# Three weight units without a part of x, and two steps in another order, in a gated-experts kernel

## The chip, the core and the metric

The kernel runs on one core of one Trainium2 chip. The metric is device time in microseconds (us), from the start to the end of one execution. Shown are the median of three runs and one execution taken by the hardware profiler, whose trace all rows below come from. The engines are PE (TensorE matmul), PEld (its weight loads), DVE (VectorE), ACT (ScalarE), POOL (GpSimd) and SP (SyncE); the last two only issue transfers here.

## What is computed

x has 512 rows of 64 positions with 768 columns. A score per position (x times aw) is turned into a softmax over the 64 positions, and the weighted sum of the positions is the feature of the row. The feature goes through four gate networks and eight experts of two layers; each row takes the gate of its own head D, and the experts' outputs are summed with that gate.

```python
p = softmax(where(x.sum(-1) != 0, einsum('bld,d->bl', x, aw), -inf))
feature = einsum('bl,bld->bd', p, x)
g_all = softmax(relu(feature @ gW1[h] + gb1) @ gW2[h] + gb2);  gate = g_all[arange(b), D]
h1 = relu((feature @ eW1[e] + eb1) * inv1 + bn1_b)
h2 = relu((h1 @ eW2[e] + eb2) * inv2 + bn2_b)
rep = einsum('be,ebo->bo', gate, h2)
out = softmax((rep @ hW[h] + hb)[arange(b), D])
```

## The kernel before

x is read in 32 **rounds** of 16 rows (8 tiles of 128 positions x 768). DVE multiplies each tile by aw and sums it (`score_tiles`, L626, tile prod_out); ACT sums each tile for the mask (`sum_rows`, L429, copy_out). Then DVE masks the scores (`mask_scores`, L632, L636), PE transposes them (`turn_scores`, L915), DVE takes the maximum (`softmax_max`, L641, neg_max), ACT the exponential (L436), DVE normalises (`softmax_norm`, L647 recip and L649 prob), PE transposes the result (`turn_probs`, L919), ACT spreads it into pwin (`place_probs`, L447), and PE adds the weighted rows to the feature sum (`add_features`, L937, 32 matmul rows in the trace). Eight rounds make a block of 128 rows. After a block ACT and DVE each copy half of the sum (`copy_rows`, L452, L655), PE transposes it (`turn_features`, L950), ACT and DVE split it into a high and a low part (`features_hi` L457, `features_lo` L661).

The batch is worked in two chunks of 256 rows. The weights of a chunk come in **units** of 128 x 3 x 384 elements, 56 for each chunk, 112 in all. Nearly every unit is split in two parts: ACT writes whi (`split_hi`, L414), DVE the rest wlo (`split_lo`, L614), and PE makes three products for each tile: 27 matmuls a unit (L875, L876, L877). The second-layer units of the first three experts of chunk 0 are not split (L906). The first-layer output h1 of an expert is split by DVE the same way, in two halves (`split_h1`, L682 h1_hi and L684 h1_lo). `add_expert` (L702, L706) multiplies an expert's output by its gate and adds it to rep; `pick_gate` (L692) readies the gate's broadcast, which PE makes (L961). POOL issues the weights' transfers into four raw buffers, each as soon as `split_lo` has read the buffer's last unit (L394); SP issues those of x into a ring of four rounds, each when `add_features` has freed a round.

The program has two stretches. The first works rounds 0 to 15 with x alone. The second has one **slot** for each unit: 112 slots, written out by hand in each engine's queue. In slot s PE multiplies unit s, while ACT and DVE split unit s + 2 (AHEAD = 2; there are three pairs of split buffers, so `split_hi(s + 2)` waits until PE has used unit s - 1). The slots also carry x: each takes a third of a round (three, three and two tiles), so rounds 16 to 31 end in slot 46. Which third a slot carries is

```python
SLOT_THIRD = THIRDS * FIRST_ROUNDS + 1
r, third = divmod(SLOT_THIRD + s, THIRDS)
```

(L147; L562 for ACT, L832 for DVE, L1025 for PE). Third 0 has the masking, and on PE `add_features` of two rounds earlier and then `turn_scores`; third 1 has the maximum and the exponential; third 2 has `softmax_norm` on DVE and, behind the unit on PE, `turn_probs`. So PE's queue waits in every third slot for DVE's L649.

In a DVE slot the order is: first tile, the softmax step, `split_lo(s + 2)` (L847), `split_h1` where H1_SLOT has one (L848), the other tiles, then `gate_norm`, `gate_set`, `pick_gate`, `add_expert`. Chunk 0 has slots 0 to 55. Its second-layer units of expert 7 are units 54 and 55; unit 56 is the first gate unit of chunk 1, and PE waits before it for the features of blocks 2 and 3. Block 3 is complete with round 31, whose sum PE makes in slot 50 (BLOCK_SLOT, L153). The gate of a chunk takes five steps in the slots behind its eight gate units: logits, copy, pick, norm, set (L139). PE transposes the gate behind the unit of the slot in which DVE makes the norm (`turn_gate`, L997, waits for L761), and DVE sets it in the next slot (`gate_set`, L771, L773). HEAD_SLOT = gate_at(1) + 12 is where PE makes chunk 0's last product.

Of the kernel before, what the change touches and what calls it, by code (L numbers as in the profile page):

```python
# [21 lines left out]
BLOCK_ROUNDS = 8  # L22
RAW = 4
SPLIT = 3
AHEAD = 2
# [8 lines left out]
THIRDS = 3  # L34


def rec_kernel(nc, x, D, aw, gW1, gb1, gW2, gb2, eW1, eb1, bn1_g, bn1_b, eW2, eb2, bn2_g, bn2_b, hW, hb, out):
    B, L, DM = x.shape
    H, _, HD = gW1.shape
# [4 lines left out]
    CB = CHUNK // P  # L44
    NBLK = B // P
    ROUNDS = NBLK * BLOCK_ROUNDS
# [7 lines left out]
    with ExitStack() as ctx:  # L54
# [22 lines left out]
        SLOTS = len(UNITS)  # L77
# [58 lines left out]
        def gate_at(c):  # L136
            return unit_of(c, "g", 0, 0)

        GATE_LOGITS, GATE_COPY, GATE_PICK, GATE_NORM, GATE_SET = (  # L139
            {gate_at(c) + n: c for c in range(NCH)} for n in (2 * H, 2 * H + 1, 2 * H + 2, 2 * H + 3, 2 * H + 4))  # L140
        HEAD_SLOT = gate_at(1) + 2 * H + 4

        FIRST_ROUNDS = CB * BLOCK_ROUNDS
        SLOT_THIRD = THIRDS * FIRST_ROUNDS + 1  # L147

        def to_score(third):
            return range(3 * third, min(3 * third + 3, ROUND_TILES))  # L150


        BLOCK_SLOT = {THIRDS * (BLOCK_ROUNDS * (b + 1) + 1) - SLOT_THIRD: b for b in range(CB, NBLK)}  # L153
        assert max(BLOCK_SLOT) + 3 < gate_at(1)

        xring = sb("xring", [P, RING_ROUNDS, CG, 2, DM])
        aw_bc = sb("aw_bc", [P, DM])
# [246 lines left out]
        def _(act):  # L404
# [154 lines left out]
                features_hi(1, g)  # L559

            for s in range(SLOTS):
                r, third = divmod(SLOT_THIRD + s, THIRDS)  # L562
                if s - 1 in BLOCK_SLOT:
                    copy_rows(BLOCK_SLOT[s - 1])
                if r <= ROUNDS:
                    split_hi(s + AHEAD)
                if s:
                    read_panel(s - 1, (2,))
                if r > ROUNDS:
                    split_hi(s + AHEAD)  # L570
                if s - 2 in BLOCK_SLOT:
                    for g in range(2):
                        features_hi(BLOCK_SLOT[s - 2], g)
                if s in GATE_NORM:
                    gate_exp(GATE_NORM[s])

                ts = to_score(third) if r < ROUNDS else ()
                sum_rows(r, ts[:1])
                if third == 0 and FIRST_ROUNDS <= r - 2 < ROUNDS:
                    place_probs(r - 2)  # L580
                sum_rows(r, ts[1:2])
                if third == 1 and FIRST_ROUNDS < r <= ROUNDS:
                    softmax_exp(r - 1)
                sum_rows(r, ts[2:])
                read_panel(s, (0, 1))
                if s == HEAD_SLOT + 1:
                    head_exp(0)
# [4 lines left out]
        def _(dve):  # L592
# [17 lines left out]
            def split_lo(u):  # L610
                if u >= SLOTS or not is_split(u):
                    return
                dve.wait_ge(hi_ready, SPLITS[u])
                nc.vector.tensor_tensor(wlo[:, split_slot(u), :, :], wraw[:, raw_slot(u), :, :],  # L614
                                        whi[:, split_slot(u), :, :].bitcast(F32), ALU.subtract).then_inc(lo_ready, 1)

            def score_tiles(r, ts):
                for t in ts:
                    j, i = divmod(t, 2)
                    if i == 0:  # L620
                        dve.wait_ge(x_loaded[r % RING_ROUNDS][j], x_count(r))
                    at = r * ROUND_TILES + t
                    if at >= 2:

                        dve.wait_ge(scored, at - 1)
                    nc.vector.tensor_tensor_reduce(  # L626
                        out=prod_out[:, t % 2, :], in0=xring[:, r % RING_ROUNDS, j, i, :], in1=aw_bc[:, :], scale=1.0,
                        scalar=0.0, op0=ALU.mult, op1=ALU.add, accum_out=score[:, r % 2, t:t + 1]).then_inc(scored, 1)
# [37 lines left out]
            def split_h1(c, q, half):  # L666

                n = SPLIT_EXPERT_AT[(c, q)]
                if n and q == 0:

                    dve.wait_ge(logits_ready, c + 1)
                elif n:
                    pc, pq = SPLIT_EXPERTS[n - 1]
                    wait_unit_used(dve, unit_of(pc, "c", pq, half))
                elif NATIVE:

                    wait_unit_used(dve, unit_of(0, "c", NATIVE - 1, 1))
                else:
                    dve.wait_ge(logits_ready, 1)
                dve.wait_ge(z_read, tiles(panel_of(c, "ab"[half], q), MT - 1))  # L680
                ks = slice(KU * half, KU * half + KU)
                nc.vector.tensor_copy(h1_hi[:, ks, :], h1[:, ks, :]).then_inc(h1_hi_ready, 1)  # L682
                dve.wait_ge(h1_hi_ready, h1_count(c, q, half))
                nc.vector.tensor_tensor(h1_lo[:, ks, :], h1[:, ks, :], h1_hi[:, ks, :].bitcast(F32),  # L684
                                        ALU.subtract).then_inc(h1_ready, 1)
# [79 lines left out]
            def gate_set(c):  # L765
                dve.wait_ge(gate_turned, c + 1)
                if c:

                    dve.wait_ge(gate_bc_ready, E * c)

                nc.vector.tensor_copy(gateT[0:E, :], turn_ps[0:E, 0:CHUNK]).then_inc(gateT_hi_ready, 1)  # L771
                dve.wait_ge(gateT_hi_ready, c + 1)
                nc.vector.tensor_tensor(gateT[LOW:LOW + E, :], turn_ps[0:E, 0:CHUNK], gateT[0:E, :].bitcast(F32),  # L773
                                        ALU.subtract).then_inc(gateT_ready, 1)
# [54 lines left out]
                features_lo(1, g)  # L829

            for s in range(SLOTS):
                r, third = divmod(SLOT_THIRD + s, THIRDS)  # L832
                if s in GATE_COPY:
                    gate_copy(GATE_COPY[s])
                if s in GATE_PICK:
                    gate_pick(GATE_PICK[s])
                if s - 1 in BLOCK_SLOT:
                    copy_rows(BLOCK_SLOT[s - 1])
                ts = to_score(third) if r < ROUNDS else ()
                score_tiles(r, ts[:1])  # L840
                if third == 0 and r <= ROUNDS:
                    mask_scores(r - 1)
                if third == 1 and FIRST_ROUNDS < r <= ROUNDS:
                    softmax_max(r - 1)
                if third == 2 and FIRST_ROUNDS < r <= ROUNDS:
                    softmax_norm(r - 1)
                split_lo(s + AHEAD)  # L847
                for c, q, half in H1_SLOT.get(s, ()):  # L848
                    split_h1(c, q, half)
                score_tiles(r, ts[1:])  # L850
                if s - 2 in BLOCK_SLOT:
                    for g in range(2):
                        features_lo(BLOCK_SLOT[s - 2], g)
                if s in GATE_NORM:
                    gate_norm(GATE_NORM[s])
                if s in GATE_SET:
                    gate_set(GATE_SET[s])
                if s == HEAD_SLOT + 1:
                    head_pick(0)

                    nc.vector.memset(rep[:, :, :], 0.0).then_inc(rep_zeroed, 1)
                if s == HEAD_SLOT + 2:
                    head_norm(0)
                if s in PICK_SLOT:
                    pick_gate(*PICK_SLOT[s])
                if s in ADD_SLOT:
                    add_expert(*ADD_SLOT[s])
# [5 lines left out]
        def _(pe):  # L873
# [148 lines left out]
            turn_features(1)  # L1022

            for s in range(SLOTS):
                r, third = divmod(SLOT_THIRD + s, THIRDS)  # L1025
                if s in (gate_at(c) for c in range(NCH)):

                    pe.wait_ge(feat_ready, 2 * CB * (UNITS[s][0] + 1))
                unit(s)
                if s in GATE_LOGITS:  # L1030
                    gate_logits(GATE_LOGITS[s])
                if s in GATE_COPY:
                    turn_gate_logits(GATE_COPY[s])
                if s in GATE_NORM:
                    turn_gate(GATE_NORM[s])
                if s == HEAD_SLOT:
                    head_logits(0)
                if s - 1 in PICK_SLOT:
                    gate_broadcast(*PICK_SLOT[s - 1])
                if third == 0 and FIRST_ROUNDS <= r - 2 < ROUNDS:  # L1040
                    add_features(r - 2)
                if third == 0 and r <= ROUNDS:
                    turn_scores(r - 1)
                if third == 2 and FIRST_ROUNDS < r <= ROUNDS:
                    turn_probs(r - 1)
                if s - 1 in BLOCK_SLOT:
                    turn_features(BLOCK_SLOT[s - 1])
# [27 lines left out]
```

## Time and profile before

| | |
|---|---|
| median of three runs | 601.56 us (601.42 to 602.04) |
| the profiled execution | 601.48 us |
| span of its trace, first to last instruction | 599.7 us |
| PE busy | 509.0 us (85%), 4191 instructions |
| DVE busy | 482.8 us (81%), 961 |
| ACT busy | 455.3 us (76%), 1007 |
| POOL busy | 81.3 us (14%), 118 |
| moved by DMA | 168.05 MB, mean 280 GB/s |

The profiled execution's own time is 1.8 us over its span. Times in the rows below are counted from the start of the span. The first stretch ends near 140 us, x ends near 360 us, and the rest is weights alone. A busy share is an average over these stretches, so each is read by itself. PE's matmuls overlap, and the profile models their ends: the distance from one start to the next tells what one costs.

### The profile page before, as it was taken

How to read it: one execution, taken by the hardware profiler on the slowest of the kernel's cores; microseconds unless marked ns; L12 is line 12 of the kernel's file. 1: busy time of each engine (PE TensorE's matmuls, PEld its weight loads, DVE VectorE, ACT ScalarE, POOL GpSimd, SP SyncE). 2: the span in 40 equal slices, each digit the busy share in tenths (PEclk: the TensorE clock that was granted, in tenths of full speed). 3: DMA queues.
4: the chain of work that ended last, by engine and by line, in shares of the span. 5: the costliest groups of instructions: out<-in, count | busy, mean ns of one | idle time of the engine just before them, and what ended most of it. 6: DMA issues, size and time to landing. Idle time of an engine off the chain costs nothing.

```text
span 599.7 us, 11283 instructions
## 1 busy us (share of the span) xinstructions
PE 509.0 (85%) x4191; PEld 416.2 (69%) x4191; DVE 482.8 (81%) x961; ACT 455.3 (76%) x1007; POOL 81.3 (14%) x118
## 2 busy tenths in 40 slices
PE   0456555746999999999998989999999999999995
PEld 0111121212978787887777878889999999999995
DVE  6989999997899898888999999475376766667664
ACT  5989999996899888988999986555545665665651
POOL 0000000001112020210111111111211222221200
PEclk9987897698899999999999989999999999999998
DMA  8999999989999999999899944455555566566520
GB/s 315 400 364 402 401 401 401 389 337 385 405 392 395 386 391 394 385 385 354 326 346 347 334 118 155 123 182 157 175 160 155 172 190 193 166 191 187 170 81 0
DMA packets 52339, 168.05 MB, mean 280 GB/s; under 512 B 4797, under 2 KB 5041, under 8 KB 52285
## 3 DMA queue, kind: packets, MB, share of 16 engines
q1 hardware_dynamic: 36012, 100.88, 44.1%
q0 software_dynamic: 16128, 66.07, 33.6%
q8 instruction: 33, 0.54, 0.4%
q10 hardware_dynamic: 144, 0.39, 0.2%
q14 instruction: 22, 0.17, 0.1%
HBM read 167.32 MB, written 0.00 MB: 279 GB/s over the span
## 4 chain that ended last, share of the span: by engine, by line
PE 52%; DVE 23%; DMA 11%; issue 8%; ACT 4%; SPq 1%; ACTq 0%; DVEq 0%
DVE prod_out L626 15%; PE z_ps L875 14%; PE z_ps L876 14%; PE z_ps L877 14%; DMA xring<-in_r_x_dram 11%; PE feat_ps L937 4%; PE z_ps L906 4%; DVE wlo L614 3%; ACT copy_out L429 2%; ACT whi L414 2%; DVE h_hi L682 1%; DVE score L626 0%; SPq L355 0%; DVE h L702 0%; DVE feat_lo L661 0%
## 5 line engine op out<-in xcount | busy, mean ns | idle before, releaser
L626 DVE CUSTOM_DVE_ANT_0 prod_out<-xring,aw_bc 128x768 bf16<-128x768 f32 x256 | 233.2, 947 | 7.1 <-DMA xring<-in_r_x_dram 6.5
L429 ACT ACTIVATE copy_out<-xring 128x768 bf16<-128x768 f32 x256 | 212.6, 832 | 10.3 <-DMA xring<-in_r_x_dram 9.3
L875 PE MATMUL z_ps<-feat_hi,whi 128*128 128x256 f32 x720 | 207.3, 288 | 2.5 <-DVE feat_lo L661 1.2
L876 PE MATMUL z_ps<-feat_lo,whi 128*128 128x256 f32 x720 | 204.3, 284 | 0.0
L877 PE MATMUL z_ps<-feat_hi,wlo 128*128 128x256 f32 x720 | 204.2, 284 | 0.0
L614 DVE TENSOR_TENSOR wlo<-wraw,whi 128x1152 fp32r<-128x1152 f32 x106 | 143.4, 1353 | 74.5 <-ACT whi L414 73.0
L414 ACT ACTIVATE whi<-wraw 128x1152 fp32r<-128x1152 f32 x106 | 122.8, 1158 | 56.9 <-PE z_ps L877 56.1
L875 PEld LDWEIGHTS z_ps<-feat_hi,whi 128*128 128x128 f32 x720 | 139.0, 193 | 4.0 <-DVE feat_lo L661 1.6
L876 PEld LDWEIGHTS z_ps<-feat_lo,whi 128*128 128x128 f32 x720 | 138.8, 193 | 0.0
L877 PEld LDWEIGHTS z_ps<-feat_hi,wlo 128*128 128x128 f32 x720 | 138.7, 193 | 0.0
L937 PE MATMUL feat_ps<-xring,pwin 128*32 128x384 f32 x1024 | 108.4, 559 | 19.6 <-ACT pwin L447 19.6
L465 ACT ACTIVATE h<-z_ps,bias,scale 128x256 f32<-128x256 f32 x144 | 79.0, 560 | 40.0 <-PE z_ps L877 35.7
L394 POOL DMA_DIRECT2D wraw<-in_L_rec_eW_dram x90 | 67.5, 750 | 259.8 <-DVE wlo L614 253.0
L937 PEld LDWEIGHTS feat_ps<-xring,pwin 128*32 128x32 f32 x1024 | 30.8, 119 | 65.5 <-issue 39.6
L875 PE MATMUL z_ps<-h_hi,whi 128*128 128x256 f32 x234 | 67.7, 289 | 1.4 <-DVE h_lo L684 1.4
L876 PE MATMUL z_ps<-h_lo,whi 128*128 128x256 f32 x234 | 66.9, 286 | 0.0
L877 PE MATMUL z_ps<-h_hi,wlo 128*128 128x256 f32 x234 | 66.8, 286 | 0.0
L429 ACT ACTIVATION_READ_ACCUMULATOR copy_out<-xring 128x1 f32 x256 | 48.1, 188 | 0.0
L875 PEld LDWEIGHTS z_ps<-h_hi,whi 128*128 128x128 f32 x234 | 45.6, 195 | 2.2 <-issue 2.2
L876 PEld LDWEIGHTS z_ps<-h_lo,whi 128*128 128x128 f32 x234 | 45.7, 195 | 0.0
L877 PEld LDWEIGHTS z_ps<-h_hi,wlo 128*128 128x128 f32 x234 | 45.5, 195 | 0.0
L919 PE MATMUL soft_ps<-ident,prob 128*128 128x128 f32 x32 | 10.4, 324 | 33.2 <-DVE prob L649 33.1
(102 smaller groups left out, 325.9 us busy)
## 6 DMA issues: line engine op xcount, KB each, us to landing
xring<-in_r_x_dram SPq DMA_DIRECT2D x128, 768.0 KB, 8.1
wraw<-in_L_rec_eW_dram POOLq DMA_DIRECT2D x90, 576.0 KB, 4.5
wraw<-in_L_rec_gW_dram POOLq DMA_DIRECT2D x16, 576.0 KB, 4.2
w2raw<-in_L_rec_eW_dram POOLq DMA_DIRECT2D x6, 576.0 KB, 7.4
aw_bc<-in_L_rec_aw_dram ACTq DMA_DIRECT2D x1, 384.0 KB, 5.6
w2raw<-in_L_rec_gW_dram SPq DMA_DIRECT2D x1, 48.0 KB
h<-in_L_rec_eb_dram SPq DMA_DIRECT2D x1, 24.0 KB
h<-in_L_rec_bn_g_dram SPq DMA_DIRECT2D x1, 24.0 KB
```

The source lines that it names most:

```text
L394: pool.dma_start(wraw[:, raw_slot(u), :, :], src).then_inc(w_loaded[raw_slot(u)], 16)
L414: nc.scalar.activation(whi[:, split_slot(u), :, :], wraw[:, raw_slot(u), :, :], ACT.Copy).then_inc(hi_ready, 1)
L429: nc.scalar.activation(copy_out[:, t % 2, :], xring[:, r % RING_ROUNDS, j, i, :], ACT.Copy, accum_out=rowsum[:, r % 2, t:t + 1]).then_inc( ...
L465: ins = nc.scalar.activation(dest, src, ACT.Relu, bias=bias[:, col:col + 1], scale=scale[:, col:col + 1])
L614: nc.vector.tensor_tensor(wlo[:, split_slot(u), :, :], wraw[:, raw_slot(u), :, :], whi[:, split_slot(u), :, :].bitcast(F32), ALU.subtract) ...
L626: nc.vector.tensor_tensor_reduce(out=prod_out[:, t % 2, :], in0=xring[:, r % RING_ROUNDS, j, i, :], in1=aw_bc[:, :], scale=1.0, scalar=0.0 ...
L875: nc.tensor.matmul(psum_tile, w_hi, a_hi, start=first, stop=False)
L876: nc.tensor.matmul(psum_tile, w_hi, a_lo, start=False, stop=False)
L877: return nc.tensor.matmul(psum_tile, w_lo, a_hi, start=False, stop=last)
L906: last = nc.tensor.matmul(z, w2raw[:, half, k, cols], h1[:, kk, :], start=(kk == 0), stop=(kk == KT - 1))
L919: nc.tensor.transpose(soft_ps[:, P:2 * P], prob[:, :, :].rearrange("t h l -> t (h l)"), ident[:, :]).then_inc(prob_turned, 1)
L937: last = nc.tensor.matmul(feat_ps[32 * j:32 * j + 32, half, 0:DM // 2], pwin[:, 2 * j + i, at:at + 32], xring[:, r % RING_ROUNDS, j, i, DM ...
```

## The change

Three slots, 30, 36 and 42, carry no part of x: in them `third` is None, no tile is scored or summed, and no softmax step falls in them. All later thirds move back, so that x ends in slot 49 and block 3 is complete in slot 53. Second, `split_h1` goes ahead of `split_lo` in DVE's slot. Third, PE transposes the gate one slot later, DVE sets it one slot later, and HEAD_SLOT moves by one. Nothing is added to or taken from the work.

```diff
-        GATE_LOGITS, GATE_COPY, GATE_PICK, GATE_NORM, GATE_SET = (
+        GATE_LOGITS, GATE_COPY, GATE_PICK, GATE_NORM, GATE_TURN = (
             {gate_at(c) + n: c for c in range(NCH)} for n in (2 * H, 2 * H + 1, 2 * H + 2, 2 * H + 3, 2 * H + 4))
-        HEAD_SLOT = gate_at(1) + 2 * H + 4
+        HEAD_SLOT = gate_at(1) + 2 * H + 5
...
+        REST_SLOTS = (30, 36, 42)
+
+        def x_at(s):
+            at = SLOT_THIRD + s - sum(rest <= s for rest in REST_SLOTS)
+            return (at // THIRDS, at % THIRDS) if s not in REST_SLOTS else ((at + 1) // THIRDS, None)
...
-        BLOCK_SLOT = {THIRDS * (BLOCK_ROUNDS * (b + 1) + 1) - SLOT_THIRD: b for b in range(CB, NBLK)}
-        assert max(BLOCK_SLOT) + 3 < gate_at(1)
+        BLOCK_SLOT = {s: b for s in range(SLOTS) for b in range(CB, NBLK) if x_at(s) == (BLOCK_ROUNDS * (b + 1) + 1, 0)}
+        assert max(BLOCK_SLOT) + 3 <= gate_at(1)
...
-                r, third = divmod(SLOT_THIRD + s, THIRDS)
+                r, third = x_at(s)
...
-                ts = to_score(third) if r < ROUNDS else ()
+                ts = to_score(third) if r < ROUNDS and third is not None else ()
...
-                split_lo(s + AHEAD)
                 for c, q, half in H1_SLOT.get(s, ()):
                     split_h1(c, q, half)
+                split_lo(s + AHEAD)
...
-                if s in GATE_SET:
-                    gate_set(GATE_SET[s])
+                if s - 1 in GATE_TURN:
+                    gate_set(GATE_TURN[s - 1])
...
-                if s in GATE_NORM:
-                    turn_gate(GATE_NORM[s])
+                if s in GATE_TURN:
+                    turn_gate(GATE_TURN[s])
```

Two places in DVE's queue show it. Lines of the changed kernel are five higher in these functions (L619 is `split_lo`, L631 `score_tiles`, L687 and L689 `split_h1`, L707 and L711 `add_expert`). The first place is slots 41 to 43, around `add_expert` of expert 4, before:

```order
L626 ISA prod_out,score<-xring,aw_bc 128x768
L626 ISA score 128x1
L702 TENSOR_TENSOR h2<-h2,turn_ps 128x768
L706 TENSOR_TENSOR rep<-rep,h2 128x768
L626 ISA prod_out,score<-xring,aw_bc 128x768
L626 ISA score 128x1
L641 TENSOR_REDUCE neg_max<-soft_ps 8x2
L614 TENSOR_TENSOR wlo<-wraw,whi 128x1152
```

and in the change:

```order
L631 ISA prod_out,score<-xring,aw_bc 128x768
L631 ISA score 128x1
L707 TENSOR_TENSOR h2<-h2,turn_ps 128x768
L711 TENSOR_TENSOR rep<-rep,h2 128x768
L619 TENSOR_TENSOR wlo<-wraw,whi 128x1152
L631 ISA prod_out,score<-xring,aw_bc 128x768
L631 ISA score 128x1
L652 RECIPROCAL recip<-expsum 8x2
```

Slot 42 now holds one `split_lo` and nothing else, and the `add_expert` that stood ahead of a maximum stands ahead of a norm. The second place is slots 53 and 54, at the end of chunk 0, before:

```order
L614 TENSOR_TENSOR wlo<-wraw,whi 128x1152
L702 TENSOR_TENSOR h2<-h2,turn_ps 128x768
L706 TENSOR_TENSOR rep<-rep,h2 128x768
L614 TENSOR_TENSOR wlo<-wraw,whi 128x1152
L682 CAST h1_hi<-h1 128x768
L684 TENSOR_TENSOR h1_lo<-h1,h1_hi 128x768
L692 CAST pick<-sel 128x128
```

and in the change:

```order
L707 TENSOR_TENSOR h2<-h2,turn_ps 128x768
L711 TENSOR_TENSOR rep<-rep,h2 128x768
L660 COPY rows<-feat_ps 128x384
L687 CAST h1_hi<-h1 128x768
L689 TENSOR_TENSOR h1_lo<-h1,h1_hi 128x768
L619 TENSOR_TENSOR wlo<-wraw,whi 128x1152
L697 CAST pick<-sel 128x128
L619 TENSOR_TENSOR wlo<-wraw,whi 128x1152
L666 TENSOR_TENSOR feat_lo<-feat_ps,feat_hi 128x3x128 x2
```

The split of expert 7's second half of h1 now stands ahead of the `split_lo` of unit 56, and the copy and the split of block 3's features have moved in here.

## Rows read from the trace of the kernel before

**Rows 1.** Busy time by stretch: us, PE, PEld, DVE, ACT, POOL, clock, DMA share, GB/s.

```profile
314.14:342.46 28.32, 26.17 (x239) 21.85 (x231) 28.08 (x57) 25.82 (x60) 4.50 (x6) 1.00 0.93 350
...
352.40:355.80 3.40, 3.40 (x18) 3.40 (x18) 3.37 (x6) 3.37 (x8) 0.76 (x1) 0.51 0.37 87
...
500.00:525.00 25.00, 25.00 (x211) 25.00 (x210) 16.86 (x17) 14.69 (x20) 5.41 (x8) 1.00 0.60 175
```

**Rows 2.** Timeline of PE, each turn_probs of slots 28 to 49 but one.

```profile
280.85 0.33 PE L919 MATMUL soft_ps<-ident,prob 128*128 128x128 f32 x1 [0.36 <-DVE prob L649]
...
308.24 0.33 PE L919 MATMUL soft_ps<-ident,prob 128*128 128x128 f32 x1
...
323.26 0.33 PE L919 MATMUL soft_ps<-ident,prob 128*128 128x128 f32 x1 [2.06 <-DVE prob L649]
...
336.56 0.33 PE L919 MATMUL soft_ps<-ident,prob 128*128 128x128 f32 x1
...
351.57 0.33 PE L919 MATMUL soft_ps<-ident,prob 128*128 128x128 f32 x1 [2.06 <-DVE prob L649]
...
365.97 0.27 PE L919 MATMUL soft_ps<-ident,prob 128*128 128x128 f32 x1
...
378.70 0.27 PE L919 MATMUL soft_ps<-ident,prob 128*128 128x128 f32 x1
```

**Rows 3.** Timeline of DVE, slots 35 to 38: start us, us, instruction.

```profile
315.90 0.95 DVE L702 TENSOR_TENSOR h<-h,turn_ps 128x768 f32<-128x768 f32 x1
...
317.76 0.95 DVE L626 CUSTOM_DVE_ANT_0 prod_out<-xring,aw_bc 128x768 bf16<-128x768 f32 x1
...
318.63 0.27 DVE L641 TENSOR_REDUCE neg_max<-soft_ps 8x2 f32<-8x128 f32 x1
318.84 1.34 DVE L614 TENSOR_TENSOR wlo<-wraw,whi 128x1152 fp32r<-128x1152 f32 x1
...
322.74 0.15 DVE L647 RECIPROCAL recip<-expsum 8x2 f32<-8x2 f32 x1
...
323.13 1.34 DVE L614 TENSOR_TENSOR wlo<-wraw,whi 128x1152 fp32r<-128x1152 f32 x1
324.40 0.54 DVE L682 CAST h_hi<-h 128x768 fp32r<-128x768 f32 x1
...
325.85 0.95 DVE L626 CUSTOM_DVE_ANT_0 prod_out<-xring,aw_bc 128x768 bf16<-128x768 f32 x1
...
327.61 0.17 DVE L632 TENSOR_SCALAR penalty<-rowsum 128x8 f32<-128x8 f32 x1
...
327.89 1.35 DVE L614 TENSOR_TENSOR wlo<-wraw,whi 128x1152 fp32r<-128x1152 f32 x1
```

**Rows 4.** Timeline of PE at the gate of each chunk and before unit 55.

```profile
201.39 0.38 PE L997 MATMUL turn_ps<-ident,gate 128*8 128x128 f32 x2 [0.46 <-DVE gate L761]
...
398.73 0.28 PE L877 MATMUL z_ps<-h_hi,wlo 128*128 128x256 f32 x1
...
400.43 0.36 PE L875 MATMUL z_ps<-h_hi,whi 128*128 128x256 f32 x1 [1.43 <-DVE h_lo L684]
...
445.92 0.38 PE L997 MATMUL turn_ps<-ident,gate 128*8 128x128 f32 x2 [1.23 <-DVE gate L761]
```

**Rows 5.** Timeline of DVE and PE, the gate of chunk 0: set and broadcast.

```profile
208.41 0.41 DVE L773 TENSOR_TENSOR gateT<-turn_ps,gateT 8x256 fp32r<-8x256 f32 x1
...
212.12 0.47 PE L961 MATMUL turn_ps<-gateT,pick 128*128 128x256 f32 x1
```

**Rows 6.** Timeline of ACT and DVE, the end of block 3.

```profile
384.99 0.49 ACT L452 ACTIVATE rows<-feat_ps 128x384 f32<-128x384 f32 x1 [4.21 <-PE feat_ps L937]
...
389.91 0.86 ACT L457 ACTIVATE feat_hi<-feat_ps 128x384 fp32r<-128x384 f32 x2
...
392.78 1.02 DVE L661 TENSOR_TENSOR feat_lo<-feat_ps,feat_hi 128x384 fp32r<-128x384 f32 x2
```

**Rows 7.** Weight transfers issued at L394, 268 to 362 us: issue to landing.

```profile
DMA to landing us min/median/max: 4.3/6.5/8.1
```

More of the change, by code:

```diff
@@ L831, in _ @@
             for s in range(SLOTS):
-                r, third = divmod(SLOT_THIRD + s, THIRDS)
+                r, third = x_at(s)
                 if s in GATE_COPY:
@@ L838, in _ @@
                     copy_rows(BLOCK_SLOT[s - 1])
-                ts = to_score(third) if r < ROUNDS else ()
+                ts = to_score(third) if r < ROUNDS and third is not None else ()
                 score_tiles(r, ts[:1])
@@ L1024, in _ @@
             for s in range(SLOTS):
-                r, third = divmod(SLOT_THIRD + s, THIRDS)
+                r, third = x_at(s)
                 if s in (gate_at(c) for c in range(NCH)):
```

## The prediction

> **What bounds the kernel now.** I read the busy times by stretch first, because the shares of the whole span mix three different limits. From 500 to 525 us PE and its weight loads are busy throughout and DVE for 16.86 of 25 us: PE is the limit, and 211 matmuls in 25 us, 27 to a unit, make 3.2 us a unit [rows 1]. From 314.14 to 342.46 the picture is reversed: DVE is busy for 28.08 of 28.32 us, PE for 26.17 [rows 1]. So in the last third of x DVE sets the pace.
>
> The second view is PE's own timeline at the transposes that end each period [rows 2]. Where no row names a wait, from 365.97 to 378.70, a period takes 12.73 us: three units, one feature sum and two small transposes [rows 2]. Ahead of that it is 15.02 (308.24 to 323.26), 13.30 (to 336.56), 15.01 (to 351.57) and 14.40 (to 365.97). From 280.85 to 378.70 seven periods take 97.85 us, where PE alone would need 7 x 12.73 = 89.11. The rows name what PE waits for: DVE's L649, twice with 2.06 us idle [rows 2].
>
> The third view is DVE's timeline. It shows what makes a period, from one start to the next: a `split_lo` 1.27 us (323.13 to 324.40), a tile 0.87 to 0.88 (317.76 to 318.63), `split_h1` 1.45 (324.40 to 325.85), `add_expert` 1.86 (315.90 to 317.76), maximum 0.21, norm 0.39, mask 0.28 [rows 3]. Three `split_lo`, eight tiles and the softmax steps come to 3.8 + 7.0 + 0.9 = 11.7; with one `split_h1` and one `pick_gate` (0.14) this is the 13.30 seen, and with one `split_h1` and one `add_expert` the 15.02. DVE's periods are plain sums, so it never waits there, and neither ACT nor a transfer enters.
>
> The fourth view is the remaining idle time of PE that names DVE. Before unit 55 PE starts at 400.43 after a start at 398.73, where the next would come 0.12 later: 1.58 us lost to L684 [rows 4]. At the two gates the rows show 0.46 and 1.23 us idle behind a matmul whose modelled end lies 0.28 behind its start; counted as before that is 0.62 and 1.39 [rows 4].
>
> **The change, part by part.** *The rest slots.* They remove nothing. DVE still has all of its tiles, and gets one `split_lo` of 1.27 us more for each slot by which x ends later; PE gets 3.2 us of units done in the same time. Up to slot 28 nothing differs, so I start from the norm of slot 28 and add DVE's work to the norms of the changed slots, 11.7 and what H1_SLOT, ADD_SLOT and PICK_SLOT place there. To slot 32 (rest 30): 11.7 + two `split_h1` 2.9 + features 1.0 [rows 6] + rest 1.27 = 16.9. To 35: 13.3. To 39 (rest 36): 11.7 + 1.45 + 1.86 + 0.14 + 1.27 = 16.4. To 43 (rest 42): 11.7 + 1.45 + 1.86 + 1.27 = 16.3. To 46: 13.3. To 49: 11.7 + 1.45 + 1.86 = 15.0. Sum 91.2. PE needs 12.73 for a period and 12.73 + 3.2 = 15.9 for one with a rest, in the same order 15.9, 12.7, 15.9, 15.9, 12.7, 12.7. That is less than DVE in each, so DVE sets all six, and PE waits about 1.0, 0.6, 0.5, 0.4, 0.6 and 2.3 us. From 49 to 52 no tile is left and PE sets 12.7. That is 103.9 us for 24 units. Before, the same 24 units need 97.85 + 3 x 3.2 = 107.45. The gain is 3.5 us.
>
> Against this stands the clock. After the pause before 323.26 PE ran on; after the equal one before 351.57 the granted clock was 0.51 from 352.40 to 355.80, the lower level of 1.2 GHz [rows 1, 2], and the period took 14.40 where PE at the upper level takes 12.73: 1.67 us. Before, 1.1 of these lay on the path (DVE's sum was 13.30). In the change the only long pause is the one before slot 49, 2.3 us, and behind it PE has no cover: a fall there costs the whole 1.67. One pause in two had it, and the four executions known (601.42 to 602.04) lie too close together for it to come and go. I take it as falling again, and the gain as 1.8 us. The bounds are 1.8 and 3.5.
>
> The Trainium skill, page "TensorE: Matmul & The Clock Gate", section "Why this matters for your kernels", warns of idle gaps between bursts of matmuls, and only of gaps longer than these; by that rule the clock stays up and the gain is 3.5. The pause before 323.26 agrees with it, the one before 351.57 does not.
>
> *`split_h1` first.* In the x stretch it only swaps two instructions of a full engine, so nothing. The unit needs `split_lo`'s output two slots later, 6.4 us against 1.45. In slot 54 the second half of h1 needs ACT's last tile of unit 53 and 1.5 us on DVE, while `split_lo` waits for ACT's next `split_hi`. Ahead of it h1 is ready before unit 54 has run its 3.2 us. I take the whole 1.58. Bounds: 0 if the read comes late, and 1.58.
>
> *The gates.* Behind the next unit PE asks 3.2 us later, more than either wait: 0.62 and 1.39 go. At chunk 0 the set, done at 208.41 + 0.41 = 208.82 [rows 5], moves behind a `pick_gate`, two tiles, a norm and a `split_lo`: 0.14 + 1.75 + 0.39 + 1.27 = 3.55 later, at 212.37, against a broadcast at 212.12 [rows 5]. Both follow PE when it runs earlier, so about 0.2 comes back as a wait. I count 0.4 for 0.62; bounds 0 and 0.62. At chunk 1 the broadcast is two units away. Moving HEAD_SLOT by one costs nothing, under PE's units.
>
> *Block 3's end.* It comes three slots later, straight before unit 56. From PE's last feature matmul: copies 0.5 and 0.6 (ACT and DVE, side by side) [rows 6]; unit 54 covers them and h1; the transpose starts at about 3.2 and takes 0.9; ACT's `split_hi(57)` runs beside it to 4.4; the high part 0.9 to 5.2 [rows 6]; DVE's `split_lo(57)` to 5.7; the low part 1.0 [rows 6], ready at 6.7. PE is at unit 56 at 7.4. No wait, with 0.7 to spare.
>
> Transfers: POOL's order is unchanged. In slots with h1 a raw buffer is freed 1.45 later; a transfer lands in 4.3 to 8.1 us [rows 7], and between its issue and its use lie four slots, over 12.8 us.
>
> Sum: 1.8 + 1.58 + 1.39 + 0.4 = 5.2. The profiled execution's own 601.48 gives **596.3 us**; it stands 0.08 under the median, which I neglect.
>
> **The rivals.** *The clock stays up* behind slot 49: the gain is 3.5 there, in all 6.9, and the time 594.6. For it: the pause before 323.26, which was as long. *PE is fully fed*: the rests give DVE all the lead it needs, and 97.85 - 89.11 = 8.7 and 0.62 + 1.58 + 1.39 go: 589.2. Against it, DVE's sum of 91.2. *The end of block 3 comes late*: if ACT or DVE trails by 2.5 us in slots 53 to 55, the 0.7 is used up and PE waits 1.8 at unit 56: 598.0. For it, both copies stand at the head of their queues and wait. *It does not do what it says*: the waits move with the work (h1 waits for ACT's read, the gate broadcast for the gate), and DVE's period is left as it is: 601.5. *Slower*: weights come late in the x stretch. Each of the seven slots with h1 from 29 to 46 frees a buffer 1.45 us later; if landings there took over 11.3 us (12.8 - 1.45) in place of 6.5, DVE would wait up to that 1.45 in each and pass it to PE, 10.2 us: 596.3 + 10.2 = 606.5. Against it, 8.1 was the longest [rows 7].
>
> **How the numbers follow.** Chances: the forecast 0.42, clock up 0.30, block 3 late 0.14, fully fed 0.04, nothing changes 0.05, slower 0.05. The range 593.8 to 598.5 holds the first three with 0.3 to 0.5 for the steps' roundings, and leaves out 0.14. About 0.2% (1.2 us) is what a measurement here can tell from no change. Faster by more: 0.42 + 0.30 + 0.14 + 0.04 = 0.90; within: 0.05; slower: 0.05.
>
> **What would show it.** Right: DVE still without idle time from slot 28 to 49; distances between PE's transposes of about 16.9, 13.3, 16.4, 16.3, 13.3 and 15.0; one wait of about 2.3 us before slot 49 and the lower clock behind it; no wait at either gate's transpose or at unit 55. Wrong: idle time of DVE in front of `split_lo` in that stretch; PE waiting for L666 before unit 56 or for the gate at its first broadcast; distances of 12.7 and 15.9, which would mean that DVE is no longer the limit.

## The result, and the profile after

The changed kernel takes 595.41 us, the median of four runs (595.29 to 595.77), beside 601.49 us for the kernel before, measured next to it. The ratio is 0.990, with a 95% interval from 0.9884 to 0.9915. The profiled execution took 595.40 us. It is compared here with the one of before, 601.48 us.

The head of the profile's page: the span is 6.1 us shorter, and DVE does the same work (482.8 us, 961 instructions) in it.

```profile
span 593.6 us, 11283 instructions
...
PE 514.3 (87%) x4191; PEld 416.1 (70%) x4191; DVE 482.8 (81%) x961; ACT 454.4 (77%) x1007; POOL 81.2 (14%) x118
```

The timeline of PE in the changed kernel, each `turn_probs` from slot 28 on, answers to [rows 2]. The number in square brackets is PE's idle time ahead of the row, and what released it.

```profile
281.38 0.33 PE L924 MATMUL soft_ps<-ident,prob 128*128 128x128 f32 x1 [0.36 <-DVE prob L654]
...
298.39 0.27 PE L924 MATMUL soft_ps<-ident,prob 128*128 128x128 f32 x1
...
311.47 0.33 PE L924 MATMUL soft_ps<-ident,prob 128*128 128x128 f32 x1
...
327.95 0.33 PE L924 MATMUL soft_ps<-ident,prob 128*128 128x128 f32 x1 [0.17 <-DVE prob L654]
...
344.30 0.28 PE L924 MATMUL soft_ps<-ident,prob 128*128 128x128 f32 x1
...
357.52 0.33 PE L924 MATMUL soft_ps<-ident,prob 128*128 128x128 f32 x1
...
372.54 0.33 PE L924 MATMUL soft_ps<-ident,prob 128*128 128x128 f32 x1 [2.06 <-DVE prob L654]
...
385.44 0.27 PE L924 MATMUL soft_ps<-ident,prob 128*128 128x128 f32 x1
```

From start to start these are 17.01, 13.08, 16.48, 16.35, 13.22 and 15.02 us; the prediction had 16.9, 13.3, 16.4, 16.3, 13.3 and 15.0. One long wait is left, 2.06 us before slot 49. The period behind it is 12.90, so PE ran on at its upper level.

In the first period (to slot 32) PE's last wait was not for DVE. Ahead of a product of slot 32 it stood 0.51 us for ACT, whose L470 reads finished products out of z_ps, and DVE's norm was ready when PE asked for it:

```profile
296.14 0.38 PE L880 MATMUL z_ps<-h_hi,whi 128*128 128x256 f32 x1 [0.51 <-ACT h L470]
```

DVE itself names no wait from 281 to 373 us. The busy time by stretch (us, PE, PEld, DVE, ACT, POOL, granted clock, DMA share, GB/s) shows how full PE and DVE are:

```profile
314.14:342.46 28.32, 28.09 (x250) 23.86 (x249) 28.08 (x52) 25.59 (x58) 4.49 (x6) 1.00 0.94 349
372.50:375.50 3.00, 2.96 (x25) 2.96 (x26) 2.97 (x4) 2.59 (x6) 0.00 (x0) 1.00 0.23 95
```

In the first of these windows, that of [rows 1], DVE is as full as before (28.08 of 28.32 us), and PE's share rises from 26.17 to 28.09, because PE now has the units of slots 36 and 42 to work on while DVE catches up. In the second, behind the long wait, the granted clock is 1.00, the level of 2.4 GHz.

Next, the places of [rows 4] and [rows 6] in the changed kernel: PE's gate transpose of chunk 0, the transpose of block 3's features, the first product of unit 56, and the gate transpose of chunk 1.

```profile
208.66 0.38 PE L1002 MATMUL turn_ps<-ident,gate 128*8 128x128 f32 x2
...
394.94 0.96 PE L955 MATMUL feat_ps<-ident,rows 128*128 128x128 f32 x6
...
399.10 0.28 PE L880 MATMUL z_ps<-feat_hi,whi 128*128 128x256 f32 x1
...
443.02 0.38 PE L1002 MATMUL turn_ps<-ident,gate 128*8 128x128 f32 x2
```

None of them names a wait, and the products before unit 55 follow one another without a gap. DVE's and ACT's rows for the end of block 3 are these:

```profile
391.73 0.49 ACT L457 ACTIVATE rows<-feat_ps 128x384 f32<-128x384 f32 x1 [3.25 <-PE feat_ps L942]
...
391.73 0.56 DVE L660 COPY rows<-feat_ps 128x384 f32<-128x384 f32 x1 [1.61 <-PE feat_ps L942]
...
396.27 0.85 ACT L462 ACTIVATE feat_hi<-feat_ps 128x384 fp32r<-128x384 f32 x2
...
397.68 1.01 DVE L666 TENSOR_TENSOR feat_lo<-feat_ps,feat_hi 128x384 fp32r<-128x384 f32 x2
```

The copies start at 391.73. Counted from there, the transpose follows at 3.2 us (394.94), the high part ends at 5.4, the low part at 7.0, and unit 56 starts its products at 7.4 (399.10). The prediction had 3.2, 5.2, 6.7 and 7.4.

To split the difference, I follow five markers through both programs: PE's first `turn_probs` of the second stretch, and four gate broadcasts (the third of chunk 0, its last one, the first of chunk 1, and the very last). In the kernel before:

```profile
170.48 0.27 PE L919 MATMUL soft_ps<-ident,prob 128*128 128x128 f32 x1
...
266.39 0.47 PE L961 MATMUL turn_ps<-gateT,pick 128*128 128x256 f32 x1
...
403.73 0.28 PE L961 MATMUL turn_ps<-gateT,pick 128*128 128x256 f32 x1
...
460.42 0.28 PE L961 MATMUL turn_ps<-gateT,pick 128*128 128x256 f32 x1
...
590.82 0.28 PE L961 MATMUL turn_ps<-gateT,pick 128*128 128x256 f32 x1
```

and in the changed kernel:

```profile
171.56 0.27 PE L924 MATMUL soft_ps<-ident,prob 128*128 128x128 f32 x1
...
266.92 0.47 PE L966 MATMUL turn_ps<-gateT,pick 128*128 128x256 f32 x1
...
398.98 0.28 PE L966 MATMUL turn_ps<-gateT,pick 128*128 128x256 f32 x1
...
454.27 0.28 PE L966 MATMUL turn_ps<-gateT,pick 128*128 128x256 f32 x1
...
584.67 0.28 PE L966 MATMUL turn_ps<-gateT,pick 128*128 128x256 f32 x1
```

The changed kernel is 1.08 us later at the first marker, 0.53 later at the second, then 4.75, 6.15 and 6.15 earlier. Each step less the one before it is a part of the change. The loss of 1.58 at unit 55 is gone, so the rest of the third step belongs to the x stretch. The last column does the same with the profile of a second launch of this kernel (e0 below). There the end is 0.4 us longer: from 587 to 589 us, behind the last broadcast, its granted clock was 0.74.

| part, us | predicted | profiled | second profile |
|---|---|---|---|
| up to the first `turn_probs` of the second stretch | 0 | +1.08 | +0.05 |
| gate of chunk 0 | -0.4 | -0.55 | -0.56 |
| x stretch | -1.8 (-3.5 if the clock stays up) | -3.70 | -2.18 |
| unit 55 | -1.58 | -1.58 | -1.58 |
| gate of chunk 1 | -1.39 | -1.40 | -1.40 |
| behind the last broadcast | 0 | 0.0 | +0.4 |
| span | -5.2 | -6.1 | -5.2 |

### The profile page after: what moved, and what is told of

It reads as the page before. It is cut to its first block, busy times and chain, and to the rows that moved or that the text cites. A ratio compares the mean times of both kernels' runs of the same rounds, so it can differ in the third digit from the quotient of the medians.

```text
span 593.6 us, 11283 instructions
## 1 busy us (share of the span) xinstructions
PE 514.3 (87%) x4191; PEld 416.1 (70%) x4191; DVE 482.8 (81%) x961; ACT 454.4 (77%) x1007; POOL 81.2 (14%) x118
## 4 chain that ended last, share of the span: by engine, by line
PE 56%; DVE 22%; DMA 11%; issue 7%; ACT 2%; SPq 1%; ACTq 0%; DVEq 0%
PE z_ps L880 15%; PE z_ps L881 15%; PE z_ps L882 15%; DVE prod_out L631 14%; DMA xring<-in_r_x_dram 11%; PE feat_ps L942 5%; DVE wlo L619 4%; PE z_ps L911 4%; ACT copy_out L434 1%; DVE h_hi L687 1%; DVE h L707 1%; PE turn_ps L975 0%; SPq L360 0%; DVE score L631 0%; ACT whi L419 0%
## 5 line engine op out<-in xcount | busy, mean ns | idle before, releaser
L631 DVE CUSTOM_DVE_ANT_0 prod_out<-xring,aw_bc 128x768 bf16<-128x768 f32 x256 | 233.3, 946 | 6.9 <-DMA xring<-in_r_x_dram 6.3
L619 DVE TENSOR_TENSOR wlo<-wraw,whi 128x1152 fp32r<-128x1152 f32 x106 | 143.4, 1353 | 69.8 <-ACT whi L419 69.2
L942 PE MATMUL feat_ps<-xring,pwin 128*32 128x384 f32 x1024 | 114.6, 586 | 19.2 <-ACT pwin L452 19.2
L470 ACT ACTIVATE h<-z_ps,bias,scale 128x256 f32<-128x256 f32 x144 | 78.6, 559 | 36.0 <-PE z_ps L882 31.1
L920 PEld LDWEIGHTS soft_ps<-ident,masked 128*8 128x8 f32 x32 | 2.7, 83 | 47.4 <-issue 27.1
```

What stands on the lines that cost most here:

```text
L470: ins = nc.scalar.activation(dest, src, ACT.Relu, bias=bias[:, col:col + 1], scale=scale[:, col:col + 1])
L631: nc.vector.tensor_tensor_reduce(out=prod_out[:, t % 2, :], in0=xring[:, r % RING_ROUNDS, j, i, :], in1=aw_bc[:, :], scale=1.0, scalar=0.0 ...
L942: last = nc.tensor.matmul(feat_ps[32 * j:32 * j + 32, half, 0:DM // 2], pwin[:, 2 * j + i, at:at + 32], xring[:, r % RING_ROUNDS, j, i, DM ...
```

## The experiments

The theory is the prediction's: in the x stretch DVE's plain sum sets every period, and the two orders each take a wait away. The rivals are that another engine or a transfer sets the periods, that the waits only move, and, for the difference to the profile, that the clock behind the long wait makes the two cases 594.6 and 596.3. All diffs are against the changed kernel.

**e0_after_again: the changed kernel once more**, as a yardstick for the parts.

> The changed kernel once more. Theory (DVE's sums set slots 28 to 49, and the first 1.1 us lost in the profile came from PE's clock at the start of the second stretch, not from the change): distances between the transposes from slot 28 to 49 again 17.0, 13.1, 16.5, 16.4, 13.2 and 15.0 us within 0.1; the start of unit 0 to slot 10's transpose between 46 and 48 us, free to differ from the first profile by 1 us. Rival (the change itself costs 1.1 us ahead of slot 10): that distance repeats to 0.1 us. The pause before slot 49 is 2.06 us again; whether the clock falls behind it is open, and costs 1.7 us if so.

Measured: 595.25 us (596.32, 594.56, 595.27, 595.23), ratio 0.9898 (0.9884 to 0.9911). The profiled execution is the one of 596.32. Its PE timeline has the same wait before slot 49 and a longer period behind it:

```profile
356.50 0.33 PE L924 MATMUL soft_ps<-ident,prob 128*128 128x128 f32 x1
...
371.52 0.33 PE L924 MATMUL soft_ps<-ident,prob 128*128 128x128 f32 x1 [2.07 <-DVE prob L654]
...
385.92 0.27 PE L924 MATMUL soft_ps<-ident,prob 128*128 128x128 f32 x1
```

```profile
372.50:375.50 3.00, 3.00 (x18) 3.00 (x17) 2.96 (x7) 1.58 (x4) 0.76 (x1) 0.57 0.01 3
```

The granted clock is 0.57 in these 3 us (372.50 to 375.50), near the level of 1.2 GHz, and the period is 14.40 in place of 12.90. The same code with the same pause thus kept the clock in one profile and lost it in the other, which moved the x stretch by 3.70 - 2.18 = 1.5 us. The stretch ahead of the change differs too: from unit 0's first product to slot 10's `turn_probs` it is 46.11 us here, 46.78 in the first profile and 46.13 in the kernel before. So the change itself does not cost that time, as the rival had it.

**e1_rests_only: the rest slots alone**, with both orders as before.

```diff
-        GATE_LOGITS, GATE_COPY, GATE_PICK, GATE_NORM, GATE_TURN = (
+        GATE_LOGITS, GATE_COPY, GATE_PICK, GATE_NORM, GATE_SET = (
...
+                split_lo(s + AHEAD)
                 for c, q, half in H1_SLOT.get(s, ()):
                     split_h1(c, q, half)
-                split_lo(s + AHEAD)
...
-                if s in GATE_TURN:
-                    turn_gate(GATE_TURN[s])
+                if s in GATE_NORM:
+                    turn_gate(GATE_NORM[s])
```

> Only the three rest slots. Theory (parts add): 601.5 - 3.6 = 597.9 us, with the pauses of 0.62 and 1.39 us at the gates back. Unit 55's wait comes back smaller, since block 3's transposes (0.9 us) now stand ahead of unit 55 on PE: 1.58 - 0.9 = 0.7 us, so 597.9 - 0.9 = 597.0. Rival (the rests only help together with split_h1 first): 601.5 less 0.9 at most, 600.6 us.

Measured: 599.06 us (598.43 to 599.62), ratio 0.9958 (0.9945 to 0.997). The periods are 17.14, 13.29, 16.47, 16.36, 13.21 and 15.02, then 14.40 behind a pause of 2.07 at 372.31 after which the clock fell. The waits at both gates are back in full (0.46 and 1.22); the one at unit 55 is 0.82 in place of 1.43, so the rests alone take 0.61 of it. These periods come from the rest slots; the two orders take no part in them. The fall of the clock is worth 1.5 us by e0, and makes most of what the time lies above the expected one.

**e2_h1_first_only: `split_h1` ahead of `split_lo` alone**; no rest slots, and the gates as before (their lines as in e1).

```diff
-        REST_SLOTS = (30, 36, 42)
+        REST_SLOTS = ()
```

> Only split_h1 ahead of split_lo. Theory: nothing in the x stretch (periods of 13.3 and 15.0 us stay), unit 55's 1.58 us go: 599.9 us. Rival (the order in the slot is what freed the x stretch): periods of the x stretch fall to 12.7 and the time to 596 to 597 us.

Measured: 598.27 us (597.47 to 599.09), ratio 0.9945 (0.9933 to 0.9958) against 601.32 for the kernel before, measured beside it: 3.05 us, about 1.5 more than unit 55 alone would give. The x stretch has the periods of before (14.09, 13.30, 15.01, 13.30, 15.02). The wait at unit 55 is gone, and so is the one at the gate of chunk 1, though the gate's code is that of before. DVE's rows, before:

```profile
442.75 1.36 DVE L614 TENSOR_TENSOR wlo<-wraw,whi 128x1152 fp32r<-128x1152 f32 x1 [1.65 <-ACT whi L414]
...
444.03 0.56 DVE L682 CAST h_hi<-h 128x768 fp32r<-128x768 f32 x1
...
445.69 0.17 DVE L761 TENSOR_TENSOR gate<-gexp,grec 128x16 f32<-128x16 f32 x1
```

and in e2, with PE's transpose as the last row:

```profile
439.22 0.55 DVE L687 CAST h_hi<-h 128x768 fp32r<-128x768 f32 x1
...
440.96 1.36 DVE L619 TENSOR_TENSOR wlo<-wraw,whi 128x1152 fp32r<-128x1152 f32 x1 [0.20 <-ACT whi L419]
...
442.43 0.18 DVE L766 TENSOR_TENSOR gate<-gexp,grec 128x16 f32<-128x16 f32 x1
...
442.74 0.38 PE L1002 MATMUL turn_ps<-ident,gate 128*8 128x128 f32 x2
```

Before, `split_h1` stood between `split_lo` and the norm (L760, L761) and made it 1.45 us late. In e2 it runs ahead of `split_lo`, in time in which DVE had waited for ACT: the wait of 1.65 us shrinks to 0.20. The norm is done when PE asks. The profiled execution of e2 (598.32 us) adds up against that of before: -1.58 and -1.39 for the two waits, -1.1 because the clock did not fall behind its second long pause (352.47), +0.89 at the start of the second stretch (first `turn_probs` at 171.37), in all -3.2, measured -3.16.

**e3_gate_only: the later gate transposes alone**; no rest slots, and `split_h1` behind `split_lo`.

```diff
-        REST_SLOTS = (30, 36, 42)
+        REST_SLOTS = ()
...
+                split_lo(s + AHEAD)
                 for c, q, half in H1_SLOT.get(s, ()):
                     split_h1(c, q, half)
-                split_lo(s + AHEAD)
```

> Only the gate's transposes one unit later. Theory: 0.55 us at chunk 0 and 1.40 at chunk 1 go: 599.5 us. Rival (the wait moves to the broadcast of chunk 0 and to the next unit of chunk 1): 601.0 us or more, with a wait at the first broadcast.

Measured: 598.61 us (598.32 to 599.91), ratio 0.9952 (0.9938 to 0.9966). Both gate waits are gone, and PE still waits 1.42 us at unit 55. This profile also has a fall of the clock behind the first long pause:

```profile
324.04 0.47 PE L924 MATMUL soft_ps<-ident,prob 128*128 128x128 f32 x1 [2.06 <-DVE prob L654]
...
338.38 0.27 PE L924 MATMUL soft_ps<-ident,prob 128*128 128x128 f32 x1
...
352.37 0.33 PE L924 MATMUL soft_ps<-ident,prob 128*128 128x128 f32 x1 [1.10 <-DVE prob L654]
```

```profile
325.00:328.00 3.00, 3.00 (x18) 3.00 (x18) 2.97 (x6) 2.96 (x7) 0.75 (x1) 0.61 1.03 389
```

The period with the fall (granted clock 0.61) is 14.34, the next 13.99, together 28.33. In e2, with the same slots and no fall, they are 13.30 and 15.02, together 28.32. DVE went on during the fall, so the next pause was 1.10 in place of 2.06 and the fall cost nothing. Behind that shorter pause there was no fall, where the profile of before had one that cost 1.1 us. In this execution (599.91 us) a later start of the second stretch, 171.81 in place of 170.48, takes that gain back. The median lies 0.9 us below the expected time. Runs without that late start and without a costly fall would explain it, but they have no trace, so this is not shown.

**e4_rests_late and e5_rests_early: the rests elsewhere.** One line each.

```diff
-        REST_SLOTS = (30, 36, 42)
+        REST_SLOTS = (36, 42, 48)
```

```diff
-        REST_SLOTS = (30, 36, 42)
+        REST_SLOTS = (30, 31, 32)
```

> The rests in slots 36, 42 and 48 in place of 30, 36 and 42. Theory (between slots 28 and 49 DVE's work is the same whatever the places, as long as DVE is behind PE): periods of 14.2, 13.3, 17.8, 13.3, 16.4 and 16.3 us, together 91.3 as before, no pause over 1.8 us, so the clock falls less often and the time is 594.6 us or up to 1 us more. Rival (a rest pays only where add_expert follows, the places matter): another sum, off by more than 1 us.

> The rests in slots 30, 31 and 32, one behind the other. Theory: DVE has 19.6 us of work in a period where PE needs 22.3, so DVE stands idle for about 2.7 us there; after it 15.0, 13.3, 15.0, 13.3 and 15.0. Sum 94.1 in place of 91.3, time 594.6 + 2.7 = 597.3 us, and with three pauses of 2 us up to 1.5 us more for the clock. Rival (a rest is worth the same everywhere): 595.4 us.

Measured for e4: 594.12 us (594.7, 593.84, 594.41, 591.72), ratio 0.9877 (0.9859 to 0.9894). Periods 14.09, 13.30, 17.73, 13.30, 16.47 and 16.36, in all 91.25, as DVE's sum had them. No pause of PE in these periods is longer than 0.91 us, and the clock did not fall. The rival's other sum did not come. The profiled execution was the one of 594.7; the run of 591.72 has no trace, and its cause is open.

Measured for e5: 597.93 us (595.74 to 597.93), ratio 0.994 (0.9927 to 0.9953). Periods 23.50, 13.67, 13.30, 15.02, 14.41 and 13.91, in all 93.81. Here three slots with no tile, one behind the other, let DVE run ahead by more than it can use: it stands idle 1.80 and 0.68 us for ACT's whi ahead of two `split_lo`. The first two periods, 37.17 together, were expected as 22.3 and 15.0. PE's rows for the later ones:

```profile
318.11 0.33 PE L924 MATMUL soft_ps<-ident,prob 128*128 128x128 f32 x1 [0.73 <-DVE prob L654]
...
346.43 0.33 PE L924 MATMUL soft_ps<-ident,prob 128*128 128x128 f32 x1 [2.07 <-DVE prob L654]
...
374.75 0.33 PE L924 MATMUL soft_ps<-ident,prob 128*128 128x128 f32 x1 [1.01 <-DVE prob L654]
```

The full periods come behind the rests, with pauses of 2.07 and 1.01 us. The 14.41 holds a fall of the clock (0.50 from 346.93 to 349.93 us), and the shorter pause and period behind it make up for it, as in e3. The place of a rest decides what it is worth: it must lie within the periods in which DVE is behind.

**e6_half_scores: DVE's share made smaller.** In rounds 26 to 31 the scores are made from half of the columns.

```diff
+                    n = DM // 2 if r >= 26 else DM
...
-                        out=prod_out[:, t % 2, :], in0=xring[:, r % RING_ROUNDS, j, i, :], in1=aw_bc[:, :], scale=1.0,
+                        out=prod_out[:, t % 2, 0:n], in0=xring[:, r % RING_ROUNDS, j, i, 0:n], in1=aw_bc[:, 0:n], scale=1.0,
```

> The changed kernel, but rounds 26 to 31 score only the first half of the 768 columns of each tile (the scores of these rounds leave out half of their sum). Theory (DVE limits slots 28 to 49): DVE's 48 tiles lose about 0.4 us each, 19 us in all, so PE sets the pace: six periods fall from 91.2 to about 86 us, no pause of PE at L654, and the time to about 589.5 us, or 590 to 591 if ACT becomes the next limit. Rival (ACT or transfers limit as much): 594 us or more.

Measured: 590.67 us (590.24 to 591.63), ratio 0.9829 (0.9815 to 0.9842). Three of the seven rows of PE's timeline, the first, the fourth and the last:

```profile
298.07 0.27 PE L925 MATMUL soft_ps<-ident,prob 128*128 128x128 f32 x1
...
343.08 0.27 PE L925 MATMUL soft_ps<-ident,prob 128*128 128x128 f32 x1
...
381.51 0.27 PE L925 MATMUL soft_ps<-ident,prob 128*128 128x128 f32 x1
```

None of the seven names DVE any more, and the periods between them (12.85, 16.19, 15.97, 12.85, 12.73, 12.85) are near PE's own, 12.73 without a rest and 15.9 with one. The period ahead of them, to slot 32, is still 17.02: PE waits 0.50 us for ACT's L470 there, as in the changed kernel, and DVE has idle time. So the six periods from slot 28 to 49 come to 87.6 us, where about 86 were expected. DVE was the limit of the changed kernel's stretch as a whole; in its first period ACT ended last as well.

**e7_half_sums: the same for ACT**, whose mask sums in rounds 26 to 31 take half of the columns.

```diff
-                    nc.scalar.activation(copy_out[:, t % 2, :], xring[:, r % RING_ROUNDS, j, i, :], ACT.Copy,
+                    n = DM // 2 if r >= 26 else DM
+                    nc.scalar.activation(copy_out[:, t % 2, 0:n], xring[:, r % RING_ROUNDS, j, i, 0:n], ACT.Copy,
```

> The changed kernel, but rounds 26 to 31 sum only the first half of the columns on ACT for the mask. Theory: ACT loses about 0.3 us in each of 48 tiles and nothing follows: the periods stay at 17.0, 13.1, 16.5, 16.4, 13.2 and 15.0 and the time between 594.5 and 596.3 us. Rival (ACT carries part of the limit, as its 23 of 25 us busy suggest): the sum of the periods falls by 2 us or more and the time to 593 us or less.

Measured: 594.94 us (594.46 to 595.56), ratio 0.9899 (0.9883 to 0.9914). The periods are 16.81, 13.29, 16.47, 16.28, 13.30 and 15.02, in all 91.17 beside 91.16 with the whole sums, and the pause before slot 49 is there (2.07). What moves is inside: the first period loses 0.2 us, since PE now waits for DVE there and not for ACT, and the second gets it back.

```profile
297.58 0.33 PE L925 MATMUL soft_ps<-ident,prob 128*128 128x128 f32 x1 [0.62 <-DVE prob L655]
```

ACT's wait in the first period of the changed kernel cost nothing in the sum: DVE went on meanwhile.

**e8_add_later: the last `add_expert` of the stretch out of DVE's full slots**, from slot 47 to slot 50, where no tile is left.

```diff
+        ADD_SLOT = {(50 if s == 47 else s): e for s, e in ADD_SLOT.items()}
```

> The changed kernel with add_expert of expert 5 moved from slot 47 to slot 50, behind the last tile of x. Theory: the last period falls from 15.0 to 13.2 us, the sum from 91.2 to 89.4, no pause over 1 us is left for the clock to fall behind, and the time is 594.6 - 1.8 = 592.8 us. Rival (ACT's read of expert 6, which waits for this add, holds PE at a later unit): the period falls and the gain comes back as a wait of PE, 594.6 us or more.

Measured: 592.72 us (592.28 to 593.02), ratio 0.9857 (0.9844 to 0.9871). The period before slot 49 falls from 15.02 to 13.16, by the 1.86 of the `add_expert`, and the pause from 2.06 to 0.20:

```profile
356.68 0.33 PE L925 MATMUL soft_ps<-ident,prob 128*128 128x128 f32 x1
...
369.84 0.33 PE L925 MATMUL soft_ps<-ident,prob 128*128 128x128 f32 x1 [0.20 <-DVE prob L655]
```

PE names no wait behind it until the very end (583.31 us), so the rival's wait did not come. This version does the same work as the changed kernel and has the lowest median of all that do: 1.4% under the kernel before.

**e9_gate_back: the changed kernel with the gates' transposes where they were.**

```diff
-        HEAD_SLOT = gate_at(1) + 2 * H + 5
+        HEAD_SLOT = gate_at(1) + 2 * H + 4
...
-                if s - 1 in GATE_TURN:
-                    gate_set(GATE_TURN[s - 1])
+                if s in GATE_SET:
+                    gate_set(GATE_SET[s])
...
-                if s in GATE_TURN:
-                    turn_gate(GATE_TURN[s])
+                if s in GATE_NORM:
+                    turn_gate(GATE_NORM[s])
```

> The changed kernel with the gates' transposes and HEAD_SLOT back where they were. Theory (split_h1 first has already freed chunk 1's gate, as its run alone showed): only chunk 0's 0.55 us come back, 595.3 + 0.55 = 595.8 us, and PE does not wait at chunk 1's gate. Rival (the prediction's sum): 0.55 + 1.40 come back, 597.2 us.

Measured: 596.05 us (595.9 to 597.64), ratio 0.9919 (0.9907 to 0.9932). Of the two gates only the first waits again:

```profile
201.03 0.38 PE L1002 MATMUL turn_ps<-ident,gate 128*8 128x128 f32 x2 [0.46 <-DVE gate L766]
...
440.42 0.38 PE L1002 MATMUL turn_ps<-ident,gate 128*8 128x128 f32 x2
```

In the changed kernel the later transposes are worth the wait at chunk 0 alone.

**e10_h1_back: the changed kernel with `split_h1` behind `split_lo` again.**

```diff
+                split_lo(s + AHEAD)
                 for c, q, half in H1_SLOT.get(s, ()):
                     split_h1(c, q, half)
-                split_lo(s + AHEAD)
```

> The changed kernel with split_h1 behind split_lo again. Theory: only unit 55's wait comes back, at 0.82 + 0.16 = 0.98 us as in the run of the rests alone; 595.3 + 1.0 = 596.3 us, the periods of the x stretch unchanged within 0.2 us. Rival (the order in the slot matters in the x stretch): the sum of the periods moves by more than 1 us.

Measured: 596.43 us (596.34 to 597.23), ratio 0.9919 (0.9906 to 0.9933). PE waits 0.82 us for L689 at unit 55 again, and at neither gate. It is 0.82 as in e1, not the 1.43 of [rows 4].

## Why the prediction was right, and where its steps were off

The forecast of 596.3 us came within 0.9 us, and the range held the time. That it came so near is in part luck: the profiled execution was the case of the rival *the clock stays up* (594.6), and a late start of the second stretch, which no step had, took 1.08 us of the surplus back. By its steps:

- **DVE sets the x stretch: right.** Six periods predicted as 91.2 us took 91.16. e6 takes work from DVE and five of the six periods come to PE's own, e7 takes work from ACT and the sum stays, e4 moves the rests and the periods follow DVE's sum again, and e8 takes 1.86 us from one period and gets 1.86 back. That rules out the rival in which PE is fully fed, and a transfer or ACT as the limit of the sum. But "DVE sets all six" is not exact, nor are the waits of 1.0, 0.6, 0.5, 0.4 and 0.6 us for the first five: the profile names at most 0.17 for DVE at these transposes, and in the first period PE's wait of 0.51 was for ACT.
- **The clock: the term that was mis-sized.** "I take it as falling again, and the gain as 1.8 us" was one case of two that both occur. The profiled execution shows the other one, a gain of 3.70 where the prediction had 3.5 with the clock up. The reason given for a fall each time was that four executions of before lay too close together for it to come and go. The 27 runs of the kernel before beside the experiments spread from 600.56 to 602.55, wider than those four. And e3 shows that with the slots of before a fall behind the first pause is absorbed by the next one, so there it can come and go unseen. Behind slot 49 no such cover exists. The runs of e0 spread from 594.56 to 596.32, as far apart as the prediction's two cases; but the start of the second stretch varies by as much, so without traces of those runs the spread does not show the clock.
- **1.08 us that no step had.** In the profiled execution the second stretch began later, ahead of anything that the change touches, and so the sum's miss of 1.9 at the clock showed as 0.9. In e0 the start is as before (+0.05) and the clock falls: the forecast's own case. It took 596.32, by parts that are not all the forecast's: the x stretch and the first gate gave 0.5 us more, and the end lost 0.4.
- **Unit 55: right in size.** The whole 1.58 is gone. e2 gets it alone, and e3 without it keeps the wait. But the rests share in it: with them and without `split_h1` first (e1, e10) the wait is 0.82, so they take 0.61 of the 0.9 that e1's expectation put to block 3's transposes ahead of unit 55.
- **The gates: right in sum, wrong in who earns it.** 0.55 and 1.40 went, where 0.4 and 1.39 were counted. But the 1.39 at chunk 1 was put to the later transpose alone. e2 and e9 show that `split_h1` first frees it as well, since that wait came from `split_h1` standing ahead of the norm. Either order would do; so alone each earns the 1.39, and the gains of the parts may not be added up. At chunk 0 the 0.2 expected to come back as a wait did not: neither the transpose nor the broadcast behind it names one.
- **Block 3's end: right.** The low part was ready 0.4 us before unit 56 where 0.7 was predicted, and PE did not wait. The margin is thin; a fourth rest was not tried.
- **Slower by late weights: did not occur.** DVE names no wait from 281 to 373 us. The longest landing of weights issued from 268 to 372 us was 9.2 us, against the 11.3 at which the prediction saw a loss.

## What to carry to other kernels

Where an engine works through its queue without idle time, add up its start-to-start distances for a period and compare the sum with the other engine's: slots that relieve the fuller engine are worth the difference, and only where that engine is behind. Look for work with a late due time in the fullest period and move it out, as e8 does, before adding more slack. A wait that two edits can each remove is counted once, and it pays to ask of every wait which instruction stands just ahead of the late one on its engine.

## What had not been expected of the hardware

A pause of PE of 2.06 or 2.07 us before a `turn_probs` was followed by the lower granted clock (0.50 to 0.62 over 3 us, from 1 us behind the transpose's start) in 6 cases and not in 6 others (1.00), over the profiles of before, the changed kernel, e0 to e3, e5, e7, e9 and e10. The pauses were alike in length and ended at the same kind of transpose, and one and the same code had both outcomes (the changed kernel and e0). The Trainium skill's advice on gaps (page "TensorE: Matmul & The Clock Gate", section "Why this matters for your kernels") puts longer gaps at risk than these, so the 6 falls lie outside what it warns of. What decides between the two was not tried and stays open; e4, e6 and e8, which leave no such pause, had no fall in these periods.

The start of the second stretch varies from one execution to the next, whatever the kernel: PE's first `turn_probs` in it comes between 170.12 us (e9) and 172.06 us (e10). Some of that is the granted clock there. Of the 1.08 us between the profile of before and that of the changed kernel, 0.43 are there when unit 0 starts its products (151.30 and 151.73). The rest comes behind that: from 154 to 156 us the granted clock was 0.88 in the first and 0.50 in the second, and both work through unit 0 there:

```profile
154.00:156.00 2.00, 2.00 (x17) 2.00 (x16) 2.00 (x6) 0.18 (x2) 0.22 (x1) 0.88 1.03 401
```

```profile
154.00:156.00 2.00, 2.00 (x12) 2.00 (x11) 2.00 (x5) 0.61 (x2) 0.53 (x1) 0.50 1.03 402
```
